# A residual add moves from ScalarE and GpSimd to VectorE, and its row constant to the tail

## The chip, the cores and the metric

The kernel is one program on one core of a Trainium2 chip. The metric is device time in microseconds (us); smaller is better. A core has five instruction queues, which run side by side and wait for each other by semaphores: PE is TensorE (its weight loads are shown as PEld), DVE is VectorE, ACT is ScalarE, POOL is GpSimd, and SP is SyncE, which here only issues DMAs. GpSimd issues DMAs too, the scatters.

## The reference, cut to what matters

`x` is 8 x 512 x 256 in float32. `L0_attn_ref` is a long convolution over the 512 rows (done by FFT), a residual and a layer norm with weights; `L0_ffn_ref` is a mixture of 8 experts, the two best for each row.

```python
def _layernorm(x, axis=-1, eps=1e-05):
    m = jnp.mean(x, axis=axis, keepdims=True)
    v = jnp.var(x, axis=axis, keepdims=True)
    return (x - m) / jnp.sqrt(v + eps)
...
x = x + _layernorm(_L0_attn_ref(_layernorm(x, axis=-1), ...), axis=-1)
x = x + _layernorm(_L0_ffn_ref(_layernorm(x, axis=-1), ...), axis=-1)
```

The change is in the first of the two last lines. With o the output of `_L0_attn_ref`, the value added to a row of x is o * rstd - mean * rstd: a scaled row and one constant for the row. What comes next is the layer norm of the new x, which takes the row's mean away, so the constant changes nothing there; it only matters where the new x itself is added once more, at the very end.

## The kernel before, in words

The program has four parts. **Preamble** (0 to about 109 us): the convolution's kernel is built, the rows of x are normalised. **Loop over batch rows** (109 to about 290 us): `steps(step)` unrolls step n = -1 to 10, and each of the engines has its own step(n). A batch row b is 512 rows of x, held as 128 partitions x 4 x 256; it is handled in stages, each one step later than the one before: `nxt` = n+1 (forward transform, product), `cur` = n-1 (inverse transform done, o made and added to x), `mid` = n-2 (second layer norm), `tail` = n-3 (the router's choice of experts, and the scatter of the row to `z_rows` in HBM). **Expert stage** (about 330 to 597 us): 71 tiles of 128 rows through the chosen experts. **Tail** (597 us to the end): the experts' results are read back, mixed by the weights, normalised and added to x.

The order on every engine is the order in which the program is written. The queues around the change, one full step (all line numbers are those of the kernel before):

- VectorE: r and its statistics (L896 to L902), `mult(nxt, 0)` (L821 to L824, from PSUM), o (L913, L914) and its statistics, `mult(nxt, 1)`, then 1/sd (L829) and the row constant `rs[:, 1, 4:8]` (L920, `st_o`). Behind these comes `choose(tail)`: logits (L838), the best eight (L841, L844), the one-hot pair `oh` (L848), `mask` (L851), with the statistics of `mid` filled in between (L925), then `place(tail)` (L856 to L868) and `mid`'s scales (L881).
- ScalarE: normalises r (L522), `zt` (L531), the square root for o (L426), then `dl` = o * rstd - mean * rstd in four pieces (L542, `dl_ready`), then the copy `s_sb` of half of the inverse transform from PSUM (L549), which VectorE needs for the next r, then `renormalise(mid)` (L507) and the upper half of an expert's weights (L513).
- GpSimd: `combine(nxt, 0)` and `combine(nxt, 1)` (L1108 and L1110, two each, for the complex product), then the add of dl to xs (L1130, `x1_ready`), then eight scatters of `tail` (L1138).
- TensorE: products for `nxt`, `tail` and `cur`; its next forward products stand behind the rank of `mask`.

In the tail, for each batch row, `mix(b)` on VectorE adds the mixed experts in PSUM to `acc` (L1059) and takes statistics (L1063, L1068); ScalarE takes the square root (L606); `scale(b)` on VectorE makes 1/sd (L1073) and the shift `rm[:, par, 2]` (L1075, `m_rs`); ScalarE's `close(b)` applies both (L610); `add(b)` on VectorE adds x1m, the stored new x (L1081). ScalarE's `base(b)` (L599) prepares `acc` two rows ahead. GpSimd makes the `diag` weights of the products two rows ahead (L1170), released by TensorE's products (L1366). `gate` is a semaphore increment ahead of an instruction whose address is computed. The order is mix(n+1), scale(n), add(n-1); rows 3 to 6 are in a hardware loop.

Of the kernel before, what the change touches and what calls it, by code (L numbers as in the profile page):

```python
# [17 lines left out]
F32 = mybir.dt.float32  # L18
# [7 lines left out]
P = 128  # L26
# [16 lines left out]
KB = 1024  # L43
# [20 lines left out]
def program(nc, x, fwd_tab, inv_tab, lag_tab, swap_in, phase_in, ident_in, upper_in, tile_tab, lar, aim, cre, cim,  # L64
# [8 lines left out]
    def at(name, shape, dt, off):  # L73
        return nc.alloc_sbuf_tensor_at(name, shape, dt, offset=BASE + off)
# [24 lines left out]
    dl = at("dl", [P, 4, H], F32, o0 + 62 * KB)  # L99
# [31 lines left out]
    mx = at("mx", [P, 4, 8], F32, c0 + 2176)  # L131
# [170 lines left out]
    with nc.Block() as block:  # L302
# [115 lines left out]
        def _(act):  # L418
# [96 lines left out]
            def step(n):  # L515
# [19 lines left out]
                if cur.live:  # L535

                    sigma(cur, 1)
                    act.wait_ge(sem("st_o"), cur.b + 1)
                    if not cur.first():
                        act.wait_ge(sem("x1_ready"), cur.b)  # L540
                    for k in range(4):
                        last = nc.scalar.activation(dl[:, k], o[:, k], ACT.Identity, bias=rs[:, 1, 4 + k:5 + k],  # L542
                                                    scale=rs[:, 1, k:k + 1])
                    last.then_inc(sem("dl_ready"), 1)
# [89 lines left out]
        def _(dve):  # L634
# [235 lines left out]
            def step(n):  # L870
# [37 lines left out]
                if cur.live:  # L908

                    dve.wait_ge(sem("r_norm"), cur.b + 1)  # L910
                    if not cur.first():
                        dve.wait_ge(sem("dl_ready"), cur.b)
                    do(V.tensor_tensor(o[:, :, :], r[:, :, :], lwb[:, 0].unsqueeze(1).to_broadcast([P, 4, H]), ALU.mult))  # L913
                    do(V.tensor_tensor(o[:, :, :], o[:, :, :], lwb[:, 1].unsqueeze(1).to_broadcast([P, 4, H]), ALU.add))  # L914
                    stats(lambda k: o[:, k], 1)
                if nxt.live:
                    mult(nxt, 1)
                if cur.live:
                    do(inverse(cur, 1))
                    V.scalar_tensor_tensor(rs[:, 1, 4:8], mv[1][:, :, 0], -1.0, rs[:, 1, 0:4], ALU.mult,  # L920
                                           ALU.mult).then_inc(sem("st_o"), 1)
                fill = []
# [148 lines left out]
            def scale(b, par):  # L1071
# [4 lines left out]
                                       ALU.mult).then_inc(sem("m_rs"), 1)  # L1076
# [25 lines left out]
        def _(pool):  # L1102
# [20 lines left out]
            def step(n):  # L1123
# [4 lines left out]
                if cur.live:  # L1128
                    pool.wait_ge(sem("dl_ready"), cur.b + 1)
                    G.tensor_tensor(xs[cur.b][:, :, :], xs[cur.b][:, :, :], dl[:, :, :], ALU.add).then_inc(sem("x1_ready"), 1)  # L1130
# [318 lines left out]
```

## Time and profile before

| | us |
|---|---|
| median of 3 runs (657.03 to 657.66) | 657.53 |
| the profiled execution | 655.08 |
| its span, first to last instruction | 653.4 |
| busy: PE / DVE / ACT / POOL | 483.2 / 490.4 / 329.7 / 262.9 |

The profile is one execution, so its sums are compared with 655.08 (the span and 1.68 around it), and not with the median. Busy times are sums over the whole span, in which the stages have different limits. A timeline has one row per instruction or per run of equal ones (xN, with the time from the first start to the last end); the bracket at its end is the idle time of that engine just before it and what ended it. An instruction that is held inside the engine counts as busy: its row is just longer.

### The profile page before, as it was taken

The page shows a single profiled execution, that of the slowest core. Times are in us where ns is not written, and L with a number is a line of the kernel's source. Part 1 is how long each engine was busy: PE and PEld are TensorE (multiplying, and loading weights), DVE is VectorE, ACT ScalarE, POOL GpSimd, SP SyncE. Part 2 cuts the span into 40 slices and gives each one's busy share as a digit, 9 for nine tenths or more (in the row PEclk, how much of TensorE's full clock was granted, in tenths as well). Part 3 has the DMA queues.
Part 4 walks back from the last instruction along what each step waited for, and adds up shares of the span by engine and source line. Part 5 has one row for each costly group of instructions (what it writes and reads, how often), then busy time and mean ns, then how long its engine had stood idle before and what let it go on. Part 6 is the DMA issues. An engine that isn't in the chain of part 4 may idle for free. (4 is left out here: it accounts for less than half of the span.)

```text
span 653.4 us, 12349 instructions
## 1 busy us (share of the span) xinstructions
PE 483.2 (74%) x2809; PEld 418.0 (64%) x2810; DVE 490.4 (75%) x1436; ACT 329.7 (50%) x651; POOL 262.9 (40%) x205
## 2 busy tenths in 40 slices
PE   0468499958777963630069999999999999992880
PEld 0228498847666852520058889888888888892770
DVE  7897866899999977877037787777777777771696
ACT  6974831234553556522045555555555555555385
POOL 0003544554666765578702223233232333234340
PEclk9997989998989876555569999999999999997995
DMA  6106500010100473841342222222222222214973
GB/s 194 66 0 258 193 2 1 2 63 1 65 32 35 145 298 107 305 158 51 107 172 71 66 81 73 72 74 71 81 65 80 73 72 80 65 56 162 361 254 149
DMA packets 36826, 69.55 MB, mean 106 GB/s; under 512 B 7520, under 2 KB 23648, under 8 KB 36160
## 3 DMA queue, kind: packets, MB, share of 16 engines
q1 hardware_dynamic: 30320, 51.48, 24.0%
q0 software_dynamic: 6480, 17.77, 7.6%
q8 instruction: 11, 0.18, 0.1%
q14 instruction: 15, 0.12, 0.1%
HBM read 42.02 MB, written 27.21 MB: 106 GB/s over the span
## 5 line engine op out<-in xcount | busy, mean ns | idle before, releaser
L1156 POOL DMA_INDIRECT y_rows<-y_sb,dst x71 | 76.4, 1076 | 194.8 <-DVE y_sb L1049 123.9
L1331 PE MATMUL psum<-ws,z_hl 128*128 x426 | 119.8, 417 | 0.8 <-DVE z_hl L1026 0.8
L1350 PE MATMUL psum<-ws,h_hl 128*128 x852 | 115.9, 285 | 0.1
L1350 PEld LDWEIGHTS psum<-ws,h_hl 128*128 128x128 f32 x852 | 103.5, 189 | 0.3 <-issue 0.3
L1138 POOL DMA_INDIRECT z_rows<-zn,pos x64 | 76.7, 1198 | 30.6 <-issue 17.7
L1331 PEld LDWEIGHTS psum<-ws,z_hl 128*128 128x128 f32 x426 | 76.7, 192 | 16.1 <-issue 1.5
L584 ACT CAST h_hl<-psum 128x512 fp32r<-128x512 f32 x71 | 41.7, 588 | 74.5 <-PE psum L1340 74.5
L1034 DVE TENSOR_TENSOR hb<-psum,b1r 128x512 f32<-128x512 f32 x71 | 49.1, 691 | 37.6 <-issue 34.0
L576 ACT ACTIVATE z_f<-psum,gb 128x128 f32<-128x128 f32 x142 | 57.0, 451 | 34.5 <-PE psum L1318 32.8
L1318 PE MATMUL psum<-ident,z_in 128*128 128x128 f32 x142 | 28.6, 284 | 45.9 <-DMA z_in<-z_rows 42.8
L1223 PE MATMUL psum<-pm,ft 128*128 128x256 f32 x256 | 62.3, 403 | 0.0
L590 ACT ACTIVATE hg<-hb 128x512 f32<-128x512 f32 x71 | 44.9, 632 | 34.3 <-DVE hb L1034 34.0
L1252 PE MATMUL psum<-yf,it 128*128 128x256 f32 x256 | 58.7, 385 | 0.0
L1223 PEld LDWEIGHTS psum<-pm,ft 128*128 128x128 f32 x256 | 51.7, 205 | 7.7
L1252 PEld LDWEIGHTS psum<-yf,it 128*128 128x128 f32 x256 | 48.9, 193 | 6.6
L1039 DVE TENSOR_TENSOR h_hl<-psum,h_hl 128x512 fp32r<-128x512 f32 x71 | 48.3, 680 | 0.9 <-ACT h_hl L584 0.9
L1318 PEld LDWEIGHTS psum<-ident,z_in 128*128 128x128 f32 x142 | 16.2, 143 | 50.0 <-issue 45.1
L1340 PE MATMUL psum<-ident,hg 128*128 128x128 f32 x284 | 42.6, 272 | 0.0
L1340 PEld LDWEIGHTS psum<-ident,hg 128*128 128x128 f32 x284 | 35.4, 141 | 10.0 <-issue 0.2
L1366 PE MATMUL psum<-ya,diag 128*128 (+1 forms) x128 | 30.2, 397 | 15.3 <-DMA ya<-y_rows 12.8
L1116 POOL TENSOR_TENSOR pm<-xn 128x512 f32<-128x512 f32 x8 | 10.2, 1272 | 70.3 <-ACT xn L437 70.3
L1108 POOL TENSOR_TENSOR yf<-yf,tmp 128x512 f32<-128x512 f32 x16 | 23.0, 1439 | 38.0 <-DVE tmp L824 37.9
(200 smaller groups left out, 886.7 us busy)
## 6 DMA issues: line engine op xcount, KB each, us to landing
z_in<-z_rows SPq DMA_DIRECT2D x71, 129.0 KB
w_raw<-in_dram SPq DMA_DIRECT2D x16, 512.0 KB, 5.4
ya<-y_rows SPq DMA_DIRECT2D x16, 512.0 KB, 6.3
xs<-in_dram SPq DMA_DIRECT2D x8, 512.0 KB, 5.5
x_dram<-xs SPq DMA_DIRECT2D x8, 512.0 KB
x1m<-x_dram SPq DMA_DIRECT2D x2, 2048.0 KB, 9.1
out_dram<-acc SPq DMA_DIRECT2D x8, 512.0 KB, 2.6
b1r<-in_dram SPq DMA_DIRECT2D x8, 256.0 KB
```

Of the source, the lines that this page charges most:

```text
L576: last = nc.scalar.activation(z_f[:, k], ps_z[q][:, k], ACT.Identity, bias=gb[:, 1, k:k + 1], scale=gb[:, 0, k:k + 1])
L590: nc.scalar.activation(hg[q][:, :], hb[:, :], ACT.Gelu).then_inc(sem("hg_ready"), 1)
L1034: V.tensor_tensor(hb[:, :], ps_h[q], b1r[:, bass.ds(e, 1)].rearrange("p a f -> p (a f)"), ALU.add).then_inc(sem("hb_ready"), 1)
L1039: V.tensor_tensor(h_hl[q][:, 1], ps_t[q], h_hl[q][:, 0].bitcast(F32), ALU.subtract).then_inc(sem("h_split"), 1)
L1138: pool.indirect_dma_start(z_rows, bass.IndirectOffsetOnAxis(ap=pos[tail.par][:, c, k:k + 1], axis=0), zn[buf(tail.b)][:, k], None).then_in ...
L1156: pool.indirect_dma_start(y_rows, bass.IndirectOffsetOnAxis(ap=dst[q][:, 0:1], axis=0), y_sb[q][:, :], None).then_inc(sem(f"y_out{q}"), 16)
L1223: last = TE.matmul(fw[u][c][:, k], ft[:, c, t, kt * P:(kt + 1) * P], pm[row.b][:, c, t], start=t == 0, stop=t == 1)
L1252: last = TE.matmul(iv[c][:, j * H:(j + 1) * H], it[:, c, k, j * P:(j + 1) * P], yf[row.par][:, c, k], start=k == 0, stop=k == KT - 1)
L1318: last = TE.transpose(ps_z[q][:, k], z_in[q][:, k * P:(k + 1) * P], ident[:, :])
L1331: last = TE.matmul(ps_h[q], z_hl[q][:, a, k], w_at(e1, c, k * F, F), start=n == 0, stop=n == 5)
L1340: last = TE.transpose(ps_t[q][:, k], hg[q][:, k * P:(k + 1) * P], ident[:, :])
L1350: last = TE.matmul(ps_y[q], h_hl[q][:, a, k], w_at(e2, c, 1024 + k * H, H), start=n == 0, stop=n == 11)
```

## The change

VectorE does the add itself. In each of the steps with a `cur`, behind the row constant, which now goes into `xb[:, b]` and is kept, it does four times xs = o * rstd + xs, without the constant, and signals `x1_ready`. ScalarE no longer makes dl, GpSimd no longer adds it, and the buffer dl is gone. What is stored as the new x, and normalised in `mid`, lacks the constant. In the tail `scale(b)` adds `xb` of that row to the shift that ScalarE applies, behind one more wait (`m_sh`) and a gate. (`mx`, whose place xb takes, was unused.)

```diff
@@ scalar, step(n)
                     sigma(cur, 1)
-                    act.wait_ge(sem("st_o"), cur.b + 1)
-                    if not cur.first():
-                        act.wait_ge(sem("x1_ready"), cur.b)
-                    for k in range(4):
-                        last = nc.scalar.activation(dl[:, k], o[:, k], ACT.Identity, bias=rs[:, 1, 4 + k:5 + k],
-                                                    scale=rs[:, 1, k:k + 1])
-                    last.then_inc(sem("dl_ready"), 1)
@@ vector, step(n)
                     dve.wait_ge(sem("r_norm"), cur.b + 1)
                     if not cur.first():
-                        dve.wait_ge(sem("dl_ready"), cur.b)
+                        dve.wait_ge(sem("x1_ready"), cur.b)
...
                     do(inverse(cur, 1))
-                    V.scalar_tensor_tensor(rs[:, 1, 4:8], mv[1][:, :, 0], -1.0, rs[:, 1, 0:4], ALU.mult,
+                    V.scalar_tensor_tensor(xb[:, cur.b], mv[1][:, :, 0], -1.0, rs[:, 1, 0:4], ALU.mult,
                                            ALU.mult).then_inc(sem("st_o"), 1)
+
+                    for k in range(4):
+                        last = V.scalar_tensor_tensor(xs[cur.b][:, k], o[:, k], rs[:, 1, k:k + 1], xs[cur.b][:, k], ALU.mult,
+                                                      ALU.add)
+                    last.then_inc(sem("x1_ready"), 1)
@@ vector, scale(b) in the tail
                 V.scalar_tensor_tensor(rm[:, par, 2, :], mvm[par][:, :, 0], -1.0, rm[:, par, 1, :], ALU.mult,
-                                       ALU.mult).then_inc(sem("m_rs"), 1)
+                                       ALU.mult).then_inc(sem("m_sh"), 1)
+                dve.wait_ge(sem("m_sh"), b + 1)
+                gate(dve)
+                V.tensor_tensor(rm[:, par, 2, :], rm[:, par, 2, :], xb[:, bass.ds(back(b), 1)].rearrange("p a k -> p (a k)"),
+                                ALU.add).then_inc(sem("m_rs"), 1)
@@ gpsimd, step(n)
-                if cur.live:
-                    pool.wait_ge(sem("dl_ready"), cur.b + 1)
-                    G.tensor_tensor(xs[cur.b][:, :, :], xs[cur.b][:, :, :], dl[:, :, :], ALU.add).then_inc(sem("x1_ready"), 1)
```

What stands in a row on VectorE at the end of step 3 (the first with a `tail`), before (the line numbers in these rows are each kernel's own, and the number behind a name is its buffer):

```order
L829 RECIPROCAL rs<-sd 128x4 [waits sd1]
L920 SCALAR_TENSOR_TENSOR rs<-mv_111,rs 128x4 [waits dve_seq]
L838 TENSOR_TENSOR lgs<-psum,rb_sb 128x32 [waits lg_mm,x1_ready]
L925 BN_STATS st<-xs_55 128x6
L841 MAX mx_all<-lgs 128x8 [waits dve_seq]
```

and in the changed kernel:

```order
L821 RECIPROCAL rs<-sd 128x4 [waits sd1]
L912 SCALAR_TENSOR_TENSOR xb<-mv_110,rs 128x4 [waits dve_seq]
L916 SCALAR_TENSOR_TENSOR xs_56<-o,rs,xs_56 128x256 x4
L830 TENSOR_TENSOR lgs<-psum,rb_sb 128x32 [waits lg_mm,x1_ready]
L922 BN_STATS st<-xs_55 128x6
```

The four new instructions stand behind the row constant with no wait of their own; nothing else changes its place.

On GpSimd, at the end of the same step, before:

```order
L1108 TENSOR_TENSOR yf_80<-yf_80,tmp_85 128x512 [waits mult_done]
L1110 TENSOR_TENSOR yf_80<-yf_80,tmp_85 128x512
L1130 TENSOR_TENSOR xs_56<-xs_56,dl 128x1024 [waits dl_ready]
L1138 DMA z_rows<-zn_63,pos_133 33792x258 [waits zn_ready,pos_ready]
L1138 DMA z_rows<-zn_63,pos_133 33792x258 x7
```

and in the changed kernel, where the scatters stand right behind the products:

```order
L1109 TENSOR_TENSOR yf_80<-yf_80,tmp_85 128x512 [waits mult_done]
L1111 TENSOR_TENSOR yf_80<-yf_80,tmp_85 128x512
L1136 DMA z_rows<-zn_63,pos_132 33792x258 [waits zn_ready,pos_ready]
L1136 DMA z_rows<-zn_63,pos_132 33792x258 x7
```

On VectorE in the tail, ahead of the hardware loop, scale(0) and what follows it, in the changed kernel (before, the third row is not there):

```order
L1070 RECIPROCAL rm<-rm 128x4 [waits m_sd]
L1072 SCALAR_TENSOR_TENSOR rm<-mvm_175,rm 128x4 [waits m_inv]
L1076 TENSOR_TENSOR rm<-rm,xb 128x4 [waits m_sh]
L1056 TENSOR_TENSOR acc<-acc,psum 128x1024 [waits m_sum,m_base]
L1060 BN_STATS st<-acc 128x6 [waits m_mixed]
```

ScalarE's `close` and VectorE's next mix now stand behind the added row.

## Rows read from the trace of the kernel before

**Rows 1.** Timeline, end of step 4: start us, us, engine, line, operation, tiles, count.
```profile
182.24 1.26 POOL L1108 TENSOR_TENSOR yf<-yf,tmp 128x512 f32<-128x512 f32 x1 [0.93 <-DVE tmp L824]
182.28 1.24 DVE L920 SCALAR_TENSOR_TENSOR rs<-mv,rs 128x4 f32<-128x4 f32 x1
183.44 0.18 DVE L838 TENSOR_TENSOR lgs<-psum,rb_sb 128x32 f32<-128x32 f32 x1
183.46 1.27 POOL L1110 TENSOR_TENSOR yf<-yf,tmp 128x512 f32<-128x512 f32 x1
...
185.71 2.35 POOL L1130 TENSOR_TENSOR xs<-xs,dl 128x1024 f32<-128x1024 f32 x1 [0.98 <-ACT dl L542]
185.75 2.46 DVE L848 TENSOR_TENSOR oh<-iota,mif 128x32 f32<-128x32 f32 x2
```
**Rows 2.** Groups by line, whole span: busy us, mean ns of one, idle before.
```profile
L848 DVE TENSOR_TENSOR oh<-iota,mif 128x32 f32<-128x32 f32 x16 | 13.2, 862 | 0.1
...
L920 DVE SCALAR_TENSOR_TENSOR rs<-mv,rs 128x4 f32<-128x4 f32 x8 | 7.8, 973 | 0.3
```
**Rows 3.** Timeline of steps 1 and 2.
```profile
115.06 7.07 PE L1252 MATMUL psum<-yf,it 128*128 128x256 f32 x32
...
116.45 2.17 DVE L914 TENSOR_TENSOR o<-o,lwb 128x1024 f32<-128x1024 f32 x1
...
126.82 0.69 DVE L896 TENSOR_TENSOR r<-psum,s_sb 128x512 f32<-128x512 f32 x1 [2.61 <-ACT s_sb L549]
...
144.85 0.18 DVE L829 RECIPROCAL rs<-sd 128x4 f32<-128x4 f32 x1 [1.08 <-ACT sd L426]
145.07 1.52 DVE L881 SCALAR_TENSOR_TENSOR rs<-mv,rs 128x4 f32<-128x4 f32 x1
```
**Rows 4.** Timeline at the end of step 8, and SP's longest wait after it.
```profile
269.58 1.86 DVE L859 TENSOR_TENSOR carry_b<-carry_b,msum 128x8 bf16<-128x8 bf16 x1
...
272.52 0.99 POOL L1138 DMA_INDIRECT z_rows<-zn,pos  x1 [1.10 <-DVE pos L868]
```
```profile
SPq L375 <- DMA z_rows<-zn,pos: 22.1, 1, 22.1
```
**Rows 5.** Prices: VectorE's timeline in the preamble, then groups by line and shape.
```profile
11.34 0.41 DVE L724 TENSOR_TENSOR sm<-raw 128x256 f32<-128x256 f32 x1
11.68 0.41 DVE L725 TENSOR_TENSOR sm<-raw 128x256 f32<-128x256 f32 x1
```
```profile
L777 DVE SCALAR_TENSOR_TENSOR vq<-tq,phase,mag_q 128x2048 f32<-128x2048 f32 x2 | 7.5, 3854 | 1.5 <-ACT mag_q L478 1.5
L780 DVE TENSOR_TENSOR vq<-tq,mag_q 128x2048 f32<-128x2048 f32 x2 | 7.1, 3642 | 0.0
...
L720 DVE TENSOR_SCALAR vp<-qt,phase 128x256 f32<-128x256 f32 x8 | 2.2, 344 | 0.0
...
L939 DVE TENSOR_SCALAR d_rep<-d_rep 128x256 f32<-128x256 f32 x1 | 0.3, 281 | 0.0
```
**Rows 6.** Timeline behind the loop: VectorE's weight splits and GpSimd's scatter.
```profile
294.10 8.88 DVE L833 TENSOR_TENSOR ws<-w_raw,ws 128x2048 fp32r<-128x2048 f32 x4
...
294.54 9.62 POOL L1138 DMA_INDIRECT z_rows<-zn,pos  x1 [0.30 <-issue]
```
**Rows 7.** Timeline of the tail; last, a step of the chain of waits.
```profile
614.59 0.16 DVE L1075 SCALAR_TENSOR_TENSOR rm<-mvm,rm 128x4 f32<-128x4 f32 x1
...
614.75 1.90 POOL L1170 TENSOR_TENSOR diag<-ident,wgt 128x1024 f32<-128x1024 f32 x1 [1.53 <-PE psum L1366]
614.79 2.08 ACT L610 ACTIVATE acc<-acc,rm 128x256 f32<-128x256 f32 x4 [3.41 <-DVE rm L1075]
...
620.87 1.90 POOL L1170 TENSOR_TENSOR diag<-ident,wgt 128x1024 f32<-128x1024 f32 x1 [4.23 <-PE psum L1366]
...
628.95 0.74 DVE L1075 SCALAR_TENSOR_TENSOR rm<-mvm,rm 128x4 f32<-128x4 f32 x1
```
```profile
622.06 0.09 issue
```

More of the change, by code:

```diff
@@ L98, in program @@
     o = at("o", [P, 4, H], F32, o0 + 58 * KB)
-    dl = at("dl", [P, 4, H], F32, o0 + 62 * KB)
     zt = at("zt", [P, 2, T], F32, o0 + 66 * KB)
@@ L130, in program @@
     rb_sb = at("rb_sb", [P, E], F32, c0 + 2144)
-    mx = at("mx", [P, 4, 8], F32, c0 + 2176)
+    xb = at("xb", [P, B, 4], F32, c0 + 2176)
     mi = at("mi", [P, 4, 8], U32, c0 + 2304)
```

## The prediction, made before the changed kernel was run

> **What bounds the kernel now.** I read the timeline of the two stages that the change touches, all engines at once: the loop over batch rows (109 to 273 us) and the tail (the last 45 us); first one full step of the loop. In a full step (22 us) VectorE has a single gap of about 1 us; every other engine waits for it. The reader should look at what VectorE's time is spent on at the step's end [rows 1]: a 128x4 scalar_tensor_tensor (L920) takes 1.24 us, and a pair of 128x32 products (L848) takes 2.46 us. Each of the two starts just after a GpSimd instruction on SBUF (L1108 at 182.24, L1130 at 185.71) and ends with it. The same L920 takes 0.16 us where GpSimd is silent, and L848 then 0.29 us the pair. So VectorE instructions with two inputs in SBUF stand still while GpSimd computes, and those with a PSUM input (L838, 0.18 us beside L1110) don't. Over the run L920 averages 973 ns over 8 and L848 862 ns over 16 [rows 2]: six L920 of 1.24 and two of 0.16, five pairs L848 of 2.46 and three of 0.29.
>
> This is what the change acts on: GpSimd's add L1130 is the cause of the five slow L848, and it goes.
>
> **Removed, in the loop.** Each with what becomes late next.
> - Steps 3 to 7 (one batch row each): L848 comes back to 0.29 us, 2.17 us saved in each, 10.9 us in all [rows 1, 2]. Nothing else is then late: the mask, TensorE's next products and the rest of the step follow VectorE's order as before.
> - Step 1: VectorE waits 2.61 us for s_sb until 126.82 [rows 3]. The matmuls it holds were done at 115.06 + 7.07 = 122.1, but ScalarE does the four dl first. Without them s_sb is there at 122.7 and the whole 2.61 us go.
> - Step 2: L881 takes 1.52 us behind L1130 [rows 3], 1.36 more than its 0.16, and the wait before it is 1.08 us because the square root stands behind dl and s_sb; with those gone it is the usual round trip of about 0.36. Saved 1.36 + 0.72 = 2.1 us.
> - Step 8: L859 takes 1.86 us beside L1130 instead of 0.17 [rows 4], 1.7 us saved.
> - Sum: 10.9 + 2.6 + 2.1 + 1.7 = 17.3 us on VectorE's path. ScalarE's 32 dl (590 ns each) and GpSimd's eight adds lie beside VectorE and are worth only these stalls.
>
> **Added, in the loop.** Four scalar_tensor_tensor of 128x256 with two SBUF tensors and a per-partition scalar column, in each of 8 steps, all on VectorE's path: 32 instructions. No row shows this form. Two-tensor products of 128x256 start 0.34 us apart (11.34, 11.68) [rows 5]. The scalar column adds: L720 (with a column) lasts 344 ns, L939 (without) 281 ns, so 0.06 us; from the other side L777 (scalar_tensor_tensor with a column) lasts 3854 ns and L780 (a plain product of the same size and strides) 3642 ns, 0.21 us. I take 0.06, because L720 has the operand size of the new ones, and L777 writes with long strides which may have its own cost: 0.34 + 0.065 = 0.405 us each, 1.62 us a step, 13.0 us in all. The ends are 0.34 (10.9 us) and 0.55 (17.6 us).
> The Trainium skill, VectorE: DVE Perf Modes, section The TRN2 errata, gives 58 cycles plus one per element at 0.96 GHz; by it an instruction would be 0.33 us, an estimate from that page, the loop would gain 6.8 us and the total would be 1.8 us below the median. The spacing in rows 5 is what I use.
>
> **Who gets the port behind L920.** In steps 1 to 6, L920 waits for GpSimd's L1108, runs at its end, and L1110 is due at once (183.46) while the first new instruction is due at 183.44 [rows 1]. The question is whether VectorE keeps the port through five back-to-back instructions. The nearest row: four products L833 follow one another for 8.88 us without any stretch (4 x 2.2), and a GpSimd scatter that began 0.44 us into them needed 9.62 us instead of 0.96 [rows 6]. It waited through three changes from one VectorE instruction to the next and got nothing. So I let VectorE keep the port; L1110 then ends 1.6 us later, at 186.3, before L848 comes (about 187.4), and its result is read by TensorE half a step later. Cover: 1 us there; if it is gone, L848 waits for that remainder.
>
> The loop: 13.0 - 17.3 = **-4.3 us**. GpSimd's scatters after the loop run back to back from 272.5 on and the stage behind them (SP waits 22.1 us for them [rows 4]) starts with their end. Their first waits for VectorE's step 8, so the 4.3 us are passed on whole.
>
> **Added, in the tail.** In each of 8 scale() calls, between L1075 and ScalarE's L610, VectorE now waits for m_sh, does a semaphore increment (gate) and adds a 128x4 pair from SBUF. ScalarE waits for that, and behind it on VectorE stand add(), the next mix() and so TensorE. In the last 35 us the chain of waits goes through L1075 every time. Price alone: the step through the gate is about 0.14 us (the 0.09 of issue behind DVEq L241 is most of it [rows 7]) and 0.16 for the add: 0.30 us, and some 0.06 more for the register of the column in the four calls inside the hardware loop.
> But the add has two SBUF inputs too, and GpSimd makes the diag tiles here (L1170, 1.90 us). Call 0: L1075 ends at 614.75, exactly when a diag product starts [rows 7]. The add is due at 614.9 and finds the port taken until 616.6, so L610 starts at 616.7, not 614.79: 1.9 us. Call 1: ScalarE's chain is 1.9 us late, so L1075 comes at 621.2 instead of 619.26, into the next diag product (620.87 to 622.77, released by TensorE, which isn't late): 1.4 us more and the add's 0.3. Both were free in the kernel before. Call 2: 0.3. Calls 3 to 6: 0.36 each, but call 3 loses the 0.58 us that L1075 was held there (0.74 at 628.95), since the last diag product is then over. Call 7: 0.3. Sum: 1.9 + 1.7 + 0.3 + 1.4 - 0.6 + 0.3 = **+5.0 us**. Bounds: 2.6 us if no diag product is met, 6 if a third is.
>
> **Sum.** -4.3 + 5.0 = +0.7 us. The rows are of an execution of 655.08 us (span 653.4), which lies 2.45 below the median 657.53 of the runs; the difference is added to the median: **658.2 us**, +0.1%. A measurement of this kernel tells about 0.2% (1.3 us) from no change.
>
> **Rivals.**
> *B, the port changes hands at every instruction.* Place: behind L920 in steps 1 to 6. L1110, waiting since 183.46, takes the port when L920 leaves it, and the first new instruction waits about 1.1 us (until 184.6). The loop then costs 6 x 1.1 more, -4.3 + 6.6 = +2.3, with the tail +7.3: 664.8 us, slower. It decides as soon as a waiting GpSimd instruction gets in between two VectorE instructions. For it: L1108 does get in between L913 and L914 at 115.36 (L914 2.17 us behind it) [rows 3], but those two have a wait between them. Against it: rows 6. The Trainium skill, SBUF — State Buffer, section SBUF: two separate sides, says that whichever engine starts first has the shared pair for the whole instruction, nothing of keeping it for the next; read instruction by instruction it speaks for B and for 664.8, while rows 6 speak against. That a GpSimd operation is held out wholly while it waits, rows 6 show too.
> *C, the tail is cheaper.* If the first diag product falls 0.3 us later against L1075 (TensorE slower), calls 0 and 1 meet none: tail +2.6, total -1.7: 655.8 us, faster. Against it: both are released by TensorE's products, so their distance hardly varies.
> *D, the new instruction's price at its ends* (with VectorE keeping the port): 0.34 us gives 658.2 - 2.1 = 656.1, 0.55 gives 662.8.
> *E, it doesn't do what it says:* the compiled program shows the four instructions in place, dl gone from ScalarE and the add from GpSimd; what is left is that another wait holds VectorE in the loop (TensorE's products come 0.2 us late once already), so that the gain there shrinks to 2 us: 660.5.
>
> **Chances.** Forecast with its spread (D within it) 0.62, B 0.22, C 0.1, E 0.06. Within the forecast the price of the new instruction leaves about 0.18 under -1.3 us, 0.45 within and 0.37 over. Faster: 0.62 x 0.18 + 0.07 of C = 0.18. Slower: 0.62 x 0.37 + 0.21 of B + 0.04 of E = 0.48. Same: 0.34. Range 8 in 10: from 654.8 (cheap instruction with C) to 665.2 (B), since leaving B out would leave more than 2 in 10.
>
> **What would show it.** L848's successor has no member over 0.4 us; the new instructions' starts are 0.40 apart; L1110's successor lasts 2.8 us or so in steps 1 to 6 where VectorE keeps the port, and if it is 1.27 and the first new instruction lasts 1.6, B holds. VectorE reaches step 8's end 4.3 us earlier (272.2 less 4.3). In the tail the first new 128x4 add lasts 1.8 us, the second L1075 about 1.5, the others 0.16, and from 614.6 to the end it takes 5 us more than the 39 of before. Wrong would be the forecast if the loop's gain were under 2 or over 7 us, or if the diag products didn't meet the adds.

## The result

| | us |
|---|---|
| kernel before, median of 5 runs (655.58 to 657.66) | 657.03 |
| changed kernel, median of 5 runs (658.82 to 661.38) | 660.2 |
| ratio, changed to before | 1.0048, 95% interval 1.0028 to 1.0068 |
| profiled execution of the changed kernel (before: 655.08) | 658.82 |
| its span (before: 653.4) | 657.2 |

The change makes the kernel slower by 0.5%, some 3 us; the interval is clear of no change. The forecast was +0.7 us.

### The loop, after

The end of step 4 in the changed kernel's timeline (columns as in [rows 1]; L912 is the former L920, L1109 and L1111 are GpSimd's combines, L840 is the former L848, and L916 is the new add):

```profile
183.29 0.17 DVE L821 RECIPROCAL rs<-sd 128x4 f32<-128x4 f32 x1
183.46 1.26 POOL L1109 TENSOR_TENSOR yf<-yf,tmp 128x512 f32<-128x512 f32 x1 [0.94 <-DVE tmp L816]
183.50 1.25 DVE L912 SCALAR_TENSOR_TENSOR xb<-mv,rs 128x4 f32<-128x4 f32 x1
184.66 2.75 DVE L916 SCALAR_TENSOR_TENSOR xs<-o,rs,xs 128x256 f32<-128x256 f32 x4
184.68 1.26 POOL L1111 TENSOR_TENSOR yf<-yf,tmp 128x512 f32<-128x512 f32 x1
...
189.64 0.27 DVE L840 TENSOR_TENSOR oh<-iota,mif 128x32 f32<-128x32 f32 x2
```

The instructions of L916 one by one, as the view of the tile xs gives them (count; duration in ns least/median/most; first and last start), in steps 4, 5, 7 and 8:

```profile
L916 DVE SCALAR_TENSOR_TENSOR xs<-o,rs,xs x4: 471/471/1559, 184.7 to 186.9; 128x256 f32<-128x256 f32 x4
L916 DVE SCALAR_TENSOR_TENSOR xs<-o,rs,xs x4: 471/471/1560, 207.4 to 209.6; 128x256 f32<-128x256 f32 x4
L916 DVE SCALAR_TENSOR_TENSOR xs<-o,rs,xs x4: 477/477/478, 249.1 to 250.3; 128x256 f32<-128x256 f32 x4
L916 DVE SCALAR_TENSOR_TENSOR xs<-o,rs,xs x4: 476/476/478, 269.0 to 270.2; 128x256 f32<-128x256 f32 x4
```

The pair L840 takes 0.27 us where it took 2.46 [rows 1]: what was to be removed is gone. But the first new instruction lasts 1.56 us and the other three 0.47. L1111 started 0.02 us behind it and ran its full speed (1.26 us): as I read it, the port that both need was GpSimd's, and VectorE stood still for 1.09 us. The experiments test this. In steps 7 and 8, where GpSimd has no combine at that place, all four last 0.48.

Steps 1 and 2, which answer to [rows 3]:

```profile
122.34 0.58 ACT L541 COPY s_sb<-psum 128x512 f32<-128x512 f32 x1 [1.36 <-PE psum L1250]
...
123.13 1.24 DVE L912 SCALAR_TENSOR_TENSOR xb<-mv,rs 128x4 f32<-128x4 f32 x1
124.30 2.75 DVE L916 SCALAR_TENSOR_TENSOR xs<-o,rs,xs 128x256 f32<-128x256 f32 x4
126.97 0.68 DVE L888 TENSOR_TENSOR r<-psum,s_sb 128x512 f32<-128x512 f32 x1
...
140.94 1.24 DVE L912 SCALAR_TENSOR_TENSOR xb<-mv,rs 128x4 f32<-128x4 f32 x1
142.10 2.75 DVE L916 SCALAR_TENSOR_TENSOR xs<-o,rs,xs 128x256 f32<-128x256 f32 x4
```

ScalarE's s_sb is ready by 122.9, and r follows without a wait at 126.97 (before: 126.82 after a wait of 2.61 [rows 3]). The wait went, and the five instructions fill its place and 0.15 us more. The position cast of step 8, VectorE's last act for that row's scatters, starts at 274.18; the first scatter behind it at 274.62, 2.1 us later than in the kernel before [rows 4].

Behind the loop the scatter of [rows 6] is there again, behind the same four weight splits:

```profile
296.78 8.88 DVE L825 TENSOR_TENSOR ws<-w_raw,ws 128x2048 fp32r<-128x2048 f32 x4
297.22 9.62 POOL L1136 DMA_INDIRECT z_rows<-zn,pos  x1 [0.30 <-issue]
```

### The tail, after

Calls 0 and 1 of scale() (L1072 was L1075, L1076 is the new add, L1168 is the diag product, L602 was L610), which answer to [rows 7]:

```profile
614.12 0.16 DVE L1072 SCALAR_TENSOR_TENSOR rm<-mvm,rm 128x4 f32<-128x4 f32 x1
614.26 1.90 POOL L1168 TENSOR_TENSOR diag<-ident,wgt 128x1024 f32<-128x1024 f32 x1 [1.53 <-PE psum L1364]
614.42 1.75 DVE L1076 TENSOR_TENSOR rm<-rm,xb 128x4 f32<-128x4 f32 x1
616.09 1.21 DVE L1056 TENSOR_TENSOR acc<-acc,psum 128x1024 f32<-128x1024 f32 x1
616.20 2.08 ACT L602 ACTIVATE acc<-acc,rm 128x256 f32<-128x256 f32 x4 [5.23 <-DVE rm L1076]
...
619.44 1.90 POOL L1168 TENSOR_TENSOR diag<-ident,wgt 128x1024 f32<-128x1024 f32 x1 [3.29 <-PE psum L1364]
620.68 0.68 DVE L1072 SCALAR_TENSOR_TENSOR rm<-mvm,rm 128x4 f32<-128x4 f32 x1
621.50 0.16 DVE L1076 TENSOR_TENSOR rm<-rm,xb 128x4 f32<-128x4 f32 x1
```

The 512 numbers of the add take 1.75 us because a diag product began 0.16 us ahead of it and holds the port until 616.16. In call 1 it is L1072 that meets the next one, for 0.5 us. From the start of the last scatter of y to the end the changed kernel takes 63.7 us (from 593.47), the profile of before 58.6 (from 594.78). Not all of these 5.1 us lie in the calls. The first mix of each kernel, before and after:

```profile
607.75 1.22 DVE L1059 TENSOR_TENSOR acc<-acc,psum 128x1024 f32<-128x1024 f32 x1 [16.23 <-PE psum L1366]
```
```profile
607.26 1.22 DVE L1056 TENSOR_TENSOR acc<-acc,psum 128x1024 f32<-128x1024 f32 x1 [17.08 <-PE psum L1364]
```

From there to the end it is 45.6 us before and 49.9 after: 4.3 us for the eight calls. The other 0.8 us lie ahead of the first mix, where the change has nothing.

### The profile page after: what moved, and what is told of

The parts are those of the page before. It is cut to its first block and busy times, and to the rows that moved or that the text cites. A ratio compares the mean times of both kernels' runs of the same rounds, so it can differ in the third digit from the quotient of the medians.

```text
span 657.2 us, 12350 instructions
## 1 busy us (share of the span) xinstructions
PE 487.4 (74%) x2809; PEld 421.2 (64%) x2810; DVE 497.8 (76%) x1476; ACT 314.0 (48%) x619; POOL 242.8 (37%) x197
## 5 line engine op out<-in xcount | busy, mean ns | idle before, releaser
L1221 PE MATMUL psum<-pm,ft 128*128 128x256 f32 x256 | 65.5, 419 | 0.0
L1221 PEld LDWEIGHTS psum<-pm,ft 128*128 128x128 f32 x256 | 53.9, 213 | 8.6
L1364 PEld LDWEIGHTS psum<-ya,diag 128*128 128x128 f32 x128 | 25.5, 203 | 23.4 <-issue 19.7
L1109 POOL TENSOR_TENSOR yf<-yf,tmp 128x512 f32<-128x512 f32 x16 | 23.0, 1440 | 45.4 <-DVE tmp L816 45.3
```

The costliest lines, as they stand in the source:

```text
L1221: last = TE.matmul(fw[u][c][:, k], ft[:, c, t, kt * P:(kt + 1) * P], pm[row.b][:, c, t], start=t == 0, stop=t == 1)
L1364: last = TE.matmul(ps_mix[par][:, k * H:(k + 1) * H], diag[par][:, c, k], ya[:, bass.ds(n, 1), c, k].rearrange("p a h -> p (a h)"), start= ...
```

## The experiments

Three theories stand against each other for the 3 us. *Hand-over:* the port changes sides between any two VectorE instructions when GpSimd has one ready, so the loop gains nothing and the tail's cost is left over. *The prediction's:* the loop gains 4.3 us, and the tail then has to take over 7. *A slow form:* the new instruction has a price of its own beside GpSimd, or the time is lost somewhere else. The experiments ran on three chips (1 to 4; 5 to 8; 9 to 11) and share runs of the kernel before on their own chip (medians 654.9, 655.6 and 654.7 us), so ratios are compared, not times across chips. Where a profile of an experiment is compared with the kernel before, the measure is the profile of the eighth experiment, the kernel before once more. It comes from the second chip, so such differences hold less exactly than the ratios.

### 1. The loop half alone

```diff
@@ scale(b): the changed kernel, less
-                                       ALU.mult).then_inc(sem("m_sh"), 1)
-                dve.wait_ge(sem("m_sh"), b + 1)
-                gate(dve)
-                V.tensor_tensor(rm[:, par, 2, :], rm[:, par, 2, :], xb[:, bass.ds(back(b), 1)].rearrange("p a k -> p (a k)"),
-                                ALU.add).then_inc(sem("m_rs"), 1)
+                                       ALU.mult).then_inc(sem("m_rs"), 1)
```

> The changed kernel without the add (and its wait) in the tail; so the row constant is missing from the last result. It prices the loop half of the change alone. Theory (the changed kernel's trace): the port goes to GpSimd between L912 and the first new instruction, the loop ends 1.9 to 2.1 us later than before, part of it is absorbed at the first z_in transfer (about 336 us), and the tail is as before: total 0 to +2.1 us against the kernel before, tail from the last y scatter to the end within 0.3 us of the kernel before. Rival (the prediction's own step): the loop's gain of 4.3 us is passed on: -4.3 us. Rival 2: all of the measured difference comes from the loop: +3 or more.

Measured: 655.54 us (12 runs) against 654.88; 1.0006, interval 0.9995 to 1.0018. The loop half is worth nothing that can be measured, neither the 4.3 us gain nor a loss of 3. In its profile the position cast of step 8 starts 3.0 us later than in the eighth experiment's profile of the kernel before (274.03 and 271.06), 0.3 of which came out of the preamble; the first expert product comes 2.5 us later (331.23 and 328.74); and at the last scatter of y 0.3 is left (593.06 and 592.78). The row of the third tile's flag in VectorE's timeline, in the kernel before and in this one:

```profile
334.33 0.21 DVE L1016 TENSOR_SCALAR flag<-z_in,tab_e 128x1 f32<-128x1 f32 x1 [1.82 <-DMA z_in<-z_rows]
```
```profile
336.03 0.21 DVE L1013 TENSOR_SCALAR flag<-z_in,tab_e 128x1 f32<-128x1 f32 x1 [1.03 <-DMA z_in<-z_rows]
```

The wait for z_in is 0.8 us shorter, which takes back part of the 2.5. At the first scatter of y 1.8 us are left (345.21 and 343.45). The other 1.5 disappear over the 70 tiles behind it, which take 247.9 us here and 249.3 in the kernel before; there I can't name a place. The changed kernel and the fourth experiment's have the same program up to the tail as this one, and take 247.9 and 247.7.

The first tiles vary by themselves. The fourth experiment's kernel takes 1.7 us more than this one from the first expert product to the first scatter of y (15.7 and 14.0): it waits 1.97 us for the third z_in, and its granted TensorE clock is 0.50 (1.2 GHz) until 343.3, 11.6 us behind its first expert product; here it rises to 1.00 (2.4 GHz) at 339.1, 7.8 us behind. Six products of a tile take 2.92 us at the lower level and 1.65 at the higher. So one profile's first tiles are good to some 2 us.

### 2. The tail half alone

```diff
@@ the kernel before, with a column xb of zeros; scale(b)
-                                       ALU.mult).then_inc(sem("m_rs"), 1)
+                                       ALU.mult).then_inc(sem("m_sh"), 1)
+                dve.wait_ge(sem("m_sh"), b + 1)
+                gate(dve)
+                V.tensor_tensor(rm[:, par, 2, :], rm[:, par, 2, :], xb[:, bass.ds(back(b), 1)].rearrange("p a k -> p (a k)"),
+                                ALU.add).then_inc(sem("m_rs"), 1)
```

> The kernel before with the tail's second 128x4 instruction (wait, semaphore step, add of a column of zeros) and nothing else; the result is that of the kernel before. Theory: the add meets the diag products in call 0 (lasts about 1.8 us), the second L1075 meets the next one, the others cost 0.3 us each: tail +5.0 us, total +5.0 (4.5 to 5.5). Rival: no diag product is met, 8 x 0.3: +2.4 to +2.6. Rival 2: the tail's cost hides beside the last transfers: under +1.

Measured: 658.68 us, 1.0057 (1.0040 to 1.0073): +3.7 us, between 2.6 and 4.8. The mechanism is the forecast's, in calls 0 and 1 both (L1080 is the add here, L1175 the diag product):

```profile
612.29 1.89 POOL L1175 TENSOR_TENSOR diag<-ident,wgt 128x1024 f32<-128x1024 f32 x1 [1.53 <-PE psum L1371]
612.45 1.75 DVE L1080 TENSOR_TENSOR rm<-rm,xb 128x4 f32<-128x4 f32 x1
...
618.63 1.90 POOL L1175 TENSOR_TENSOR diag<-ident,wgt 128x1024 f32<-128x1024 f32 x1 [4.45 <-PE psum L1371]
618.71 1.84 DVE L1076 SCALAR_TENSOR_TENSOR rm<-mvm,rm 128x4 f32<-128x4 f32 x1
```

In the median the size is about 1.3 us under the forecast; the eighth experiment shows that the forecast had started from a short tail. In this profile call 1 met its diag product for 1.68 us (forecast 1.4), in the changed kernel for 0.52. The two halves together are 1.0063, the whole change 1.0048: within the intervals they add up, and the tail half is all of it.

### 3. The new instructions at another place

The removed lines (the row constant and the four adds) become `residual()`, which in steps 3 to 8 runs ahead of `oh`.

```diff
@@ vector, step(n) of the changed kernel
                 if cur.live:
                     do(inverse(cur, 1))
+                    if not tail.live:
+                        residual()
-                    V.scalar_tensor_tensor(xb[:, cur.b], mv[1][:, :, 0], -1.0, rs[:, 1, 0:4], ALU.mult,
-                                           ALU.mult).then_inc(sem("st_o"), 1)
-                    for k in range(4):
-                        last = V.scalar_tensor_tensor(xs[cur.b][:, k], o[:, k], rs[:, 1, k:k + 1], xs[cur.b][:, k], ALU.mult,
-                                                      ALU.add)
-                    last.then_inc(sem("x1_ready"), 1)
...
                 if tail.live:
-                    choose(tail, iter(fill))
+                    choose(tail, iter(fill), residual if cur.live else None)
@@ choose(row, fill, before_oh=None)
                 do(V.tensor_copy(mif[:, :, :], mi[:, :, 0:2].rearrange("p t c -> p c t")), fill)
+                if before_oh:
+                    before_oh()
```

> The changed kernel with one thing moved: in the steps that also have a row in the selection (3 to 8), the row constant and the four new instructions stand behind the selection's small reads, ahead of oh, when L1111 is over. Theory (GpSimd takes the port between two VectorE instructions because it has been waiting for it): L912 no longer waits (-1.08 us in each of 4 steps), the four new ones last 1.67 us instead of 2.75 (-1.1 in each of the same steps 3 to 6), VectorE reaches the loop's end 8 to 8.7 us earlier than in the changed kernel, some 6 to 7 us earlier than before. Total against the changed kernel: up to -8.7 us if all is passed on; less where the z_in transfer has to be waited for. Rival: the four are slow for a reason of their own (2.75 us wherever they stand): no gain, since only the place changes. Rival 2: GpSimd's combine was the cover; something else then waits (TensorE's selection products come later by the 1.7 us that oh is later) and the gain is under 3 us.

Measured: 653.77 us, 0.998 (0.9968 to 0.9992), against the changed kernel's 1.0048 some 4.5 us faster. The four last 472 ns each in step 4, where they lasted 1559 and three times 471:

```profile
L916 DVE SCALAR_TENSOR_TENSOR xs<-o,rs,xs x4: 472/473/473, 185.0 to 186.2; 128x256 f32<-128x256 f32 x4
```

So no slow form; the place counts. The step from one r to the next takes 20.5 us instead of 22.3. The forecast was 2.2 less; the row that took 0.4 of it back is VectorE's cast of eight indices, 0.58 us instead of 0.14, which now runs into the second combine:

```profile
183.41 1.27 POOL L1116 TENSOR_TENSOR yf<-yf,tmp 128x512 f32<-128x512 f32 x1
...
184.12 0.58 DVE L838 CAST mif<-mi 128x8 f32<-128x8 uint32 x1
```

It ends with the combine, at 184.7. That cast has one tensor as its input, so two inputs in SBUF are not the only thing that makes an instruction wait. The Trainium skill, SBUF — State Buffer, section SBUF: two separate sides, names both kinds: those with two SBUF inputs, and those that run in a mode with both ports; by that rule, the trace agrees.

### 4. The tail's add as four column adds

```diff
@@ scale(b)
-                V.tensor_tensor(rm[:, par, 2, :], rm[:, par, 2, :], xb[:, bass.ds(back(b), 1)].rearrange("p a k -> p (a k)"),
-                                ALU.add).then_inc(sem("m_rs"), 1)
+                for k in range(4):
+                    last = V.tensor_scalar(rm[:, par, 2, k:k + 1], rm[:, par, 2, k:k + 1], xb[:, bass.ds(back(b), 1), k], None,
+                                           ALU.add)
+                last.then_inc(sem("m_rs"), 1)
```

> The changed kernel with the tail's 128x4 add written as four 128x1 adds of a per-partition column, an instruction with one tensor input. Theory (what costs is that an instruction with two tensors in SBUF waits for GpSimd's diag product): the first of call 0 starts and ends at once, the second L1072 stands still no longer than in the kernel before, but three more instructions of 0.06 to 0.16 us stand in each call: tail +2.6 + 8 x 0.2 = about +4, 1 us less than the changed kernel; the longest of the four in call 0 is under 0.3 us. Rival (any small VectorE instruction waits there, whatever its inputs): 1.7 us again in call 0, and 1 us more than the changed kernel in all.

Measured: 662.53 us, 1.0114 (1.0095 to 1.0132), the slowest of all. The expectation had the mechanism right and the sum wrong. The collision of call 0 is gone, though the diag product covers all four:

```profile
615.26 1.90 POOL L1170 TENSOR_TENSOR diag<-ident,wgt 128x1024 f32<-128x1024 f32 x1 [1.53 <-PE psum L1366]
615.44 0.58 DVE L1077 TENSOR_SCALAR rm<-rm,xb 128x1 f32<-128x1 f32 x4 [0.16 <-DVE rm L1072]
```

But four of them take 0.58 us where one add takes 0.16: +0.42 in each of 8 calls, 3.4 us, twice what I had allowed (8 x 0.2). And in call 2 the two-input instruction ahead of them meets a diag product all the same, for 1.13 us:

```profile
625.95 1.29 DVE L1072 SCALAR_TENSOR_TENSOR rm<-mvm,rm 128x4 f32<-128x4 f32 x1
```

One collision of 1.6 us was the smaller evil.

### 5. The loop's gain without the tail's cost

The third experiment's kernel with the edit of the first.

> The third experiment's kernel without the add in the tail (the row constant is missing from the last result). It tells whether a gain of the loop reaches the end. Theory: the loop's end comes 6 us earlier than in the first experiment (4 steps of 20.5 us instead of 22.3) and of this 4 to 5 us reach the end, because the stage behind starts with the scatters' end: about -5 us against the kernel before, 0.992. Rival: what is gained in the loop is waited off at the z_in transfers or in the stage behind, as some of the loop's loss was: -2 us or less.

Measured: 648.03 us, 0.9886 (0.9866 to 0.9906): -7.5 us. All of the loop's gain arrives and more than I had forecast. Against the first experiment, which differs in the order alone, it is 1.2%, 7.9 us; the first expert product comes 7.6 us earlier (323.63 and 331.23). So the way from the loop to the end is open in this direction: the rival, that the stage behind waits gains off, falls. How exactly is less sure. This kernel and the third experiment's have the same program up to the tail and the same loop (last position cast of step 8 at 266.73 and 266.90), but their last scatters of y start at 586.52 and 588.70, and the times differ by 0.9% (6 us), where the add costs about 4. So some 2 us are a matter of the single run or the chip.

### 6. The constant put back by ScalarE

```diff
@@ scalar: added to the fifth experiment's kernel, in the step behind zt
+            def constant(row):
+                act.wait_ge(sem("zn_ready"), row.b + 1)
+                act.wait_ge(sem("st_o"), row.b + 1)
+                for k in range(4):
+                    last = nc.scalar.activation(xs[row.b][:, k], xs[row.b][:, k], ACT.Identity, bias=xb[:, row.b, k:k + 1])
+                last.then_inc(sem("x1_full"), 1)
@@ sync, store_x1
-                    sp.wait_ge(sem("x1_ready"), b + 1)
+                    sp.wait_ge(sem("x1_full"), b + 1)
```

> A version meant to beat both: the late order, no add in the tail, and ScalarE adds the row constant to x in place (4 activations in each row, 0.5 us each, two steps later, in a gap of 3 us behind the products L530) before the row is stored; the layer norms that read the row without it or with it remove a row constant. Complete computation. Theory: hidden beside VectorE, since ScalarE idles 3.2 us there: the time of the fifth experiment within 1 us, about -5 us (0.992) against the kernel before and 8 us under the changed kernel. Rival: ScalarE's square root behind it (L425) comes late and holds VectorE's reciprocal in each step, or the rows' later storing holds the loads of weights behind them: over -3 us.

Measured: 647.92 us, 0.988 (0.9863 to 0.9896), the same as the fifth: the constant costs nothing where ScalarE has a gap and nobody waits for it.

### 7. GpSimd kept from waiting at the place

```diff
@@ gpsimd, step(n): added to the first experiment's kernel
                     combine(nxt, 0)
+                    if cur.live:
+                        pool.wait_ge(sem("x1_ready"), cur.b + 1)
                     combine(nxt, 1)
```

> The first experiment's kernel (no add in the tail; the row constant is missing from the last result) with one wait more: GpSimd's second pair of combines (L1109, L1111 of the second half) starts only when the four new instructions are over, so that no GpSimd instruction is waiting at any change from one VectorE instruction to the next. Theory (a waiting GpSimd instruction gets in between two back-to-back VectorE instructions): L912 lasts 0.16 and the four 1.67 us in all steps, 2.2 us saved in each of steps 1 to 6; GpSimd's pair then reaches the CAST and the selection's pair, 0.5 to 0.7 us back, and the loop's end comes 8 to 10 us earlier than in the first experiment, unless ScalarE's copy of s_sb comes late for r: its matmuls end 1.4 us behind the combine, which is within 0.2 us of the need. Rival (the four are 2.75 us for a reason of their own): no change in their duration, and the added wait only costs.

Measured: 643.90 us, 0.9828 (0.9807 to 0.9850): -11.3 us. One wait on GpSimd, nothing on VectorE. The timeline of a step of it (L1105 and L1107 are the combines), and the four of step 5 one by one:

```profile
198.38 0.16 DVE L912 SCALAR_TENSOR_TENSOR xb<-mv,rs 128x4 f32<-128x4 f32 x1
198.46 1.67 DVE L916 SCALAR_TENSOR_TENSOR xs<-o,rs,xs 128x256 f32<-128x256 f32 x4
...
200.21 1.27 POOL L1105 TENSOR_TENSOR yf<-yf,tmp 128x512 f32<-128x512 f32 x1 [2.79 <-DVE xs L916]
...
201.44 1.26 POOL L1107 TENSOR_TENSOR yf<-yf,tmp 128x512 f32<-128x512 f32 x1
...
201.95 0.78 DVE L838 CAST mif<-mi 128x8 f32<-128x8 uint32 x1
```
```profile
L916 DVE SCALAR_TENSOR_TENSOR xs<-o,rs,xs x4: 476/476/478, 198.5 to 199.7; 128x256 f32<-128x256 f32 x4
```

L912 is 0.16 and the four are 0.48 each in all eight steps: 1.08 + 1.09 = 2.17 us saved in each of steps 1 to 6, 13 in all, less 0.63 in each of steps 3 to 6, where the cast L838 is now held. VectorE reaches the position cast of step 8 at 262.86 instead of 274.03, 11.2 us earlier. The combines come out 1.9 us later against L912 and VectorE doesn't wait for what follows from them: VectorE's r (L888) has its s_sb in time.

### 8. The kernel before, once more

> The kernel before once more, for a profile from the chip of the other experiments: how far its tail (55.4 us from the last scatter of y to the end in the profile shown) and its stage of experts vary with nothing changed. Theory: the tail of 56.5 us in the first experiment, whose tail is that of the kernel before, was an encounter with GpSimd's diag product by chance of phase, so this one shows 55.4 to 56.6 us; where it is 55.4, the loop half costs the tail about 1 us by its phase.

Its time is 654.45 us in this one execution, its tail from the start of the last scatter of y to the end 60.0 us (the expectations count the same stretch from a point 3.2 us later). With it there are nine profiles whose tail has no add: 58.6 (the one that the prediction read), 60.0, 59.7, 59.9, 59.4, 59.8, and 60.1, 60.8 and 59.6 of the experiments below. The three with the add as it stands in the change have 63.7, 63.9 and 63.9. So the add costs about 4 us, and the profile before had the shortest tail of its kind. In it VectorE was held by diag products for 0.58 us in all [rows 7], in the first experiment for 1.06 in one call, and here for 1.71, in the add of x1m (1.22 us elsewhere). The rows of the last two:

```profile
622.95 1.22 DVE L1072 SCALAR_TENSOR_TENSOR rm<-mvm,rm 128x4 f32<-128x4 f32 x1
```
```profile
622.56 2.93 DVE L1081 TENSOR_TENSOR acc<-acc,x1m 128x1024 f32<-128x1024 f32 x1
```

### 9. All of it, complete

The changed kernel with the wait of the seventh experiment, the constant on ScalarE as in the sixth, and the tail of the kernel before.

> A complete version meant to beat all others: the changed kernel's own order on VectorE, GpSimd's second pair of combines behind the four new instructions as in the seventh experiment, no add in the tail, and ScalarE puts the row constant back in place before the row is stored, as in the sixth. Theory: both are independent, so the time of the seventh experiment within 1 us: 0.983 of the kernel before, about -11.5 us, -14 us against the changed kernel. Rival: ScalarE's four activations stand in the shorter step at a place where its square root (L425) is due, and cost 1 us in each step: 0.99.

Measured: 643.72 us, 0.9827 (0.9809 to 0.9844): 11.3 us under the kernel before and some 14 under the changed kernel, with nothing left out. ScalarE's part stands in a gap, and its square root behind it still waits for VectorE and not the reverse:

```profile
190.40 1.43 ACT L537 ACTIVATE zt<-psum,gb 128x512 f32<-128x512 f32 x2
191.72 1.70 ACT L514 ACTIVATE xs<-xs,xb 128x256 f32<-128x256 f32 x4
195.34 0.30 ACT L425 ACTIVATE sd<-mv,eps 128x4 f32<-128x4 f32 x1 [1.92 <-DVE mv L655]
```

### 10. The kernel before with the wait alone

```diff
@@ gpsimd, step(n) of the kernel before
                     combine(nxt, 0)
+                    if cur.live:
+                        pool.wait_ge(sem("st_o"), cur.b + 1)
                     combine(nxt, 1)
```

> The kernel before with the wait alone: GpSimd's second pair of combines starts only when L920 is over. It tells how much of the seventh experiment's gain belongs to the change at all, and how much to GpSimd's order. Theory: L920 lasts 0.16 instead of 1.24 us in steps 1 to 6, 6.5 us off VectorE's path; but the two combines and the add L1130 behind them (1.27 + 1.27 + 2.5 us) then start 1.1 us later, so the selection's pair L848 is held longer than 2.46 us, or the CAST ahead of it is held too, and gives nearly all of it back: total -2 to +1 us. Rival: the change has no part in it and the wait alone gives the 10 us of the seventh experiment.

Measured: 651.10 us, 0.9945 (0.9926 to 0.9965): -3.6 us, more than I expected. Here is its step:

```profile
179.11 0.16 DVE L920 SCALAR_TENSOR_TENSOR rs<-mv,rs 128x4 f32<-128x4 f32 x1
...
181.09 0.78 DVE L846 CAST mif<-mi 128x8 f32<-128x8 uint32 x1
...
181.80 2.35 POOL L1132 TENSOR_TENSOR xs<-xs,dl 128x1024 f32<-128x1024 f32 x1
182.13 2.17 DVE L848 TENSOR_TENSOR oh<-iota,mif 128x32 f32<-128x32 f32 x2
```

L920 gives 1.08, the cast takes 0.63 back; but L848 is held less, not more (2.17 against 2.46): the add L1132 follows the combines at once, VectorE comes later, and so sees only the add's end. I had the sign of that wrong. What matters: the wait alone gives 3.6 us, the wait and the change's loop half together 11.3. So the loop half gives 7.7 us where the hand-over of the port doesn't take it back. In the profiles only 3 of them lie in the loop (position cast of step 8 at 265.91 and 262.86); 5.5 us are there at the last scatter of y (587.84 and 582.34). What it gives behind the loop is taken up below.

### 11. The combine in four pieces

```diff
@@ gpsimd, combine(row, u) of the first experiment's kernel
-                G.tensor_tensor(yf[par][:, 1, ks], yf[par][:, 1, ks], tmp[u][:, 1], ALU.add)
+                for j in range(2):
+                    for h in range(2):
+                        hs = slice(h * H // 2, (h + 1) * H // 2)
+                        last = G.tensor_tensor(yf[par][:, 1, 2 * u + j, hs], yf[par][:, 1, 2 * u + j, hs], tmp[u][:, 1, j, hs], ALU.add)
```

> The first experiment's kernel (no add in the tail; the row constant is missing from the last result) with the combine L1111 as four instructions of a quarter each (about 0.33 us), which wait together behind L912. Theory (the port changes hands at every instruction when both engines have one ready): the delay of 1.1 us, which stands in the first of the four new instructions alone (1559 ns, the others 471), is spread: each of the four lasts 0.47 + 0.25 to 0.35 us, about 750 to 800 ns, and their sum stays 2.7 to 3 us. Rival (GpSimd, once it has the port, runs all that it has queued): the first lasts 1.5 us or more again and the others 0.47. Rival 2 (VectorE has the priority after one turn): the first is 0.8, the others 0.47, and GpSimd's last three pieces wait for the end of the four.

Its one timed execution took 652.51 us; the experiment was made for its rows, which show how the port is given. Timeline of step 4 (L1110 is the combine in four), then the four new instructions one by one in steps 4 and 7:

```profile
183.06 2.54 DVE L916 SCALAR_TENSOR_TENSOR xs<-o,rs,xs 128x256 f32<-128x256 f32 x4
183.08 2.24 POOL L1110 TENSOR_TENSOR yf<-yf,tmp 128x128 f32<-128x128 f32 x4
```
```profile
L916 DVE SCALAR_TENSOR_TENSOR xs<-o,rs,xs x4: 672/673/753, 183.1 to 184.9; 128x256 f32<-128x256 f32 x4
L916 DVE SCALAR_TENSOR_TENSOR xs<-o,rs,xs x4: 474/475/476, 246.1 to 247.3; 128x256 f32<-128x256 f32 x4
```

Where one combine waited, the first instruction lasted 1559 ns and the rest 471. Where four wait, each of the four lasts 670 to 750, 0.2 to 0.28 us over its own 0.47, and GpSimd's four stretch to 2.24 us (1.69 where they follow one another elsewhere in the step). So the two engines take turns, one instruction each. Neither rival shows: the delay isn't in the first alone, and GpSimd isn't held out to the end. The delay of each is a little under the 0.25 to 0.35 that I had written; why, the rows don't say.

## Why the prediction was right or wrong

The side was the likeliest one, slower, and the time lies in the range. But the sum had +0.7 us and the measurement is +3.2, and its step for the loop had the wrong sign: -4.3 us was forecast, and the first scatter behind the loop came 2.1 us later. That the total was near is in part luck. Its terms one by one:

- **Removed in the loop, 17.3 us: right.** L840 is 0.27 us the pair, the wait for s_sb is gone, L851 and L873 last 0.17 and 0.16.
- **Price of the new instruction, 0.405 us each, 1.62 the four: right.** Undisturbed they take 1.67.
- **"So I let VectorE keep the port": wrong, and the step that failed.** It stood on [rows 6], where a scatter waits through four VectorE instructions. The new rows show the reverse with a combine, in six steps of eight; the profile after has the scatter of 9.62 us behind the four splits as well, so both hold in one kernel. Rival B had the mechanism and its place (1.1 us in the first new instruction, steps 1 to 6) and, with +2.3 for the loop, nearly the loop's measured end (+2.1 at the first scatter). The row that should have decided was in the list: L914 of 2.17 us in [rows 3] was a GpSimd arithmetic instruction let in behind a VectorE one, the same pair of kinds as here. I set it aside for the wait between the two, and took a row of another kind of instruction.
- **"Passed on whole": wrong for the loss.** Of the 2.5 us that the loop half is late at the first expert product, about none is left in the measured time (+0.4, -0.3 to +1.2); 0.8 of it was VectorE's wait for z_in. The changed kernel itself is 2.1 us late at the first scatter of z and 1.3 us early at the last scatter of y (593.47 and 594.78). From the position cast of step 8 to the last scatter of y, the three profiles with the loop and stage of the kernel before take 322.7, 321.7 and 321.5 us, and the three with those of the changed kernel 319.3, 319.0 and 320.5: some 2 us less behind the loop, which the prediction had at nothing. Why is open. Against the first experiment, which has this too, the gains of experiments 5 and 7 arrived whole (7.9 and 11.7 us, for 7.6 and 11.4 at the first expert product).
- **Tail +5.0: mechanism right, size off by one.** The first add lasts 1.75 us (forecast 1.8), the second L1072 only 0.68 (forecast 1.5; the diag product came 0.9 us earlier against it), so the eight calls cost 4.3 us in the profile, not 5.0. The profile's tail is 5.1 us longer all the same, since 0.8 us lie ahead of the first mix: the agreement with +5.0 is chance. And this compares two executions, of which the one of before had the shortest tail of nine. Alone the add measures +3.7 us (2.6 to 4.8), and by all profiles about 4.
- **Rival B's total of 664.8** was too high by the two last points, 2 us of the loop that weren't passed on and 1 of the tail. The forecast's 658.2 was nearer to the 660.2, though the loop's step behind it was false: errors of opposite sign, of which the largest was the port (6.6 us) and the smaller were these. Rival E's 660.5 is nearest of all, by accident: the wait that it supposes in the loop doesn't show.

## What to carry to other kernels

Ahead of moving work onto an engine that shares a port, list which instruction of the other engine will be *ready* at each boundary between the moved ones: each boundary is an opening, and it costs one whole instruction of what waits. Often the remedy is not on the busy engine: one wait on the idle one, so that its work falls beside instructions that don't need the port, was worth 11.7 us here. A small correction (a row constant) belongs on an engine with a gap and off the last chain, not into eight calls at the end; and a sum that is made from one profile takes over that profile's luck, so encounters in its base need a second look.

## What the runs showed of the hardware

- In these rows VectorE and GpSimd arithmetic take turns at their shared port instruction by instruction, even when VectorE's follow back to back: 1559/471/471/471 ns with one combine waiting, 670 to 750 each with four. The Trainium skill, SBUF — State Buffer, section SBUF: two separate sides, has the lock for one instruction; that the other engine's waiting one is next is what these runs add.
- GpSimd's indirect scatter is not let in so: 9.62 us behind four VectorE instructions of 2.2 us each in the profiles of before and after, 9.4 to 10.0 in the other profiles of this case, where most scatters take 0.96. Whether it needs many turns, one of which isn't enough, is my guess and wasn't tried.
- A cast of 128x8 from uint32 to float32, with one input, waits for GpSimd as well (0.58 and 0.78 us instead of 0.15), while column adds of 128x1 (0.58 us for four, under a diag product) and the statistics of 128x256 (0.41) don't.
- The new form costs 0.40 us from start to start at 128x256; on ScalarE, adding a column to 128x256 in place takes 0.42 us in a row of four (1.70 us), where the same with a scale column takes 0.52 (2.08 us), in place (L610) or into another tile (L542).
